# Self-attention: the even steps' probabilities are normalised on ScalarE from step 40 on, and the V fills read the normed input where it lies

## The reference, cut to what matters

```
xn  = rmsnorm(x, gamma1)                              # (8, 256, 128)
q, k, v = xn @ q_w + q_b, xn @ k_w + k_b, xn @ v_w + v_b   # 16 heads of 64
q, k = rope(q), rope(k)
scores = q k^T / 8, causal
attn = softmax(scores)
attn_out = (attn @ v) @ o_w + o_b + xn
an = rmsnorm(attn_out, gamma2)
out = shared_expert(an) + routed_top3_of_31(an) + an + attn_out, then a layernorm
```

## Time and profile before

| | us |
|---|---|
| median of 3 runs | 871.24 (869.53 to 875.28) |
| the profiled execution | 871.48 |
| its span, first to last instruction | 869.7 |
| busy: TensorE, VectorE, ScalarE, POOL | 793.9, 684.6, 574.8, 559.7 |
| self-attention, first to last POOL normalisation | 441.0 to about 735 |
| L989, POOL's normalisation | 64 instructions, 94.2 in total |
| mean granted TensorE clock | 0.985 of full speed |

### The profile page before, as it was taken

How to read it: one execution, slowest core, us unless ns; L and a number is a source line. 1 busy time by engine, 2 the same in 40 slices (tenths; PEclk the granted TensorE clock), 3 DMA queues, 4 the chain that set the end, 5 groups by cost and what they waited for, 6 DMA issues and landing times.

```text
span 869.7 us, 17333 instructions
## 1 busy us (share of the span) xinstructions
PE 793.9 (91%) x5325; PEld 524.2 (60%) x5325; DVE 684.6 (79%) x2434; ACT 574.8 (66%) x1449; POOL 559.7 (64%) x630
## 2 busy tenths in 40 slices
PE   5799999999879999999899999999998888989994
PEld 2344444444456667776556676676666556888763
DVE  3788888889788998889877858868994993565687
ACT  3588778777489999998566646547653566354343
POOL 4888888888662333332476758747796988554562
PEclk9899999999999999999999999999999999999997
DMA  8300000000015111000232212231222236354112
GB/s 242 115 2 1 0 1 0 1 0 1 0 44 152 41 39 46 34 1 2 49 74 71 62 41 68 55 74 39 60 73 69 61 104 186 115 171 144 40 48 58
DMA packets 57850, 51.87 MB, mean 60 GB/s; under 512 B 11586, under 2 KB 43042, under 8 KB 57762
## 3 DMA queue, kind: packets, MB, share of 16 engines
q1 hardware_dynamic: 55394, 46.05, 19.3%
q0 software_dynamic: 2304, 4.72, 1.9%
q10 hardware_dynamic: 64, 0.02, 0.0%
HBM read 21.66 MB, written 12.32 MB: 39 GB/s over the span
## 4 chain that ended last, share of the span: by engine, by line
PE 52%; POOL 19%; DVE 13%; issue 7%; ACT 6%; another core or an unknown queue 1%; ACTq 0%; DVEq 0%; POOLq 0%
PE psum L2092 5%; PE psum L2263 5%; DVE area L1516 4%; PE psum L2125 4%; POOL area L989 4%; PE psum L2109 4%; PE psum L2400 3%; PE psum L2420 3%; PE psum L2460 3%; PE psum L2151 3%; POOL area L898 3%; PE psum L2322 3%; PE psum L2438 3%; POOL slot_in L977 2%; PE psum L1976 2%
## 5 line engine op out<-in xcount | busy, mean ns | idle before, releaser
L989 POOL TENSOR_TENSOR area<-area,rinv 128x512 f32<-128x512 f32 x64 | 94.2, 1473 | 65.2 <-DVE rinv L1837 64.8
L1298 ACT ACTIVATE area<-area,negmax 128x128 f32<-128x128 f32 (+1 forms) x256 | 112.8, 444 | 15.6 <-DVE negmax L1516 15.6
L1145 ACT ACTIVATE area<-area,negmax 128x256 f32<-128x256 f32 x256 | 108.8, 505 | 0.0
L1516 DVE CUSTOM_DVE_ANT_0 area<-psum,area 128x256 f32<-128x256 f32 x256 | 93.2, 420 | 18.3 <-PE psum L2077 17.5
L1505 DVE SCALAR_TENSOR_TENSOR area<-psum,ccol,cs 128x1024 f32<-128x1024 f32 x64 | 81.4, 1272 | 22.8 <-PE psum L2125 22.5
L1516 DVE CUSTOM_DVE_ANT_0 area<-psum,maskc 128x128 f32<-128x128 f32 (+1 forms) x256 | 76.0, 352 | 13.0 <-PE psum L2151 9.5
L2092 PE MATMUL psum<-ident,area 128*128 128x128 f32 x512 | 70.6, 278 | 8.7 <-DVE area L1556 7.3
L2125 PE MATMUL psum<-area,qkw 128*128 128x512 f32 x128 | 71.6, 641 | 6.5 <-DVE area L1505 3.7
L1288 ACT ACTIVATE area<-psum 128x512 f32<-128x512 f32 x32 | 19.1, 598 | 75.7 <-PE psum L2460 67.7
L2092 PEld LDWEIGHTS psum<-ident,area 128*128 128x128 f32 x512 | 56.6, 142 | 18.1 <-issue 11.0
L2438 PEld LDWEIGHTS psum<-ident,area 128*128 128x128 f32 x384 | 44.7, 141 | 36.2 <-issue 25.1
(11 more groups left out here) (315 smaller groups left out, 2091.9 us busy)
## 6 DMA issues: line engine op xcount, KB each, us to landing
area<-area SPq DMA_DIRECT2D x256, 64.0 KB
slot_out<-area SPq DMA_DIRECT2D x17, 256.0 KB
area<-slot_in SPq DMA_DIRECT2D x8, 512.0 KB, 4.1
slot_in<-gate SPq DMA_DIRECT2D x5, 768.0 KB, 4.7
area<-in_L_ffn_re_w SPq DMA_DIRECT2D x14, 256.0 KB
area<-in_mask_BxSxS_ik SPq DMA_DIRECT2D x8, 256.0 KB, 3.8
area<-in_L_attn_W SPq DMA_DIRECT2D x5, 256.0 KB, 6.3
area<-in_x SPq DMA_DIRECT2D x4, 256.0 KB, 3.3
```

Source lines behind the costliest of these rows:

```text
L989: pool.tensor_tensor(p4, p4, rinv[:, u % 4, 0:4].unsqueeze(2).to_broadcast([128, 4, w]), ALU.mult)\
L1145: last = act.activation(P[:, n % 4, r, mm, :], P[:, n % 4, r, mm, :], ACT.Exp, bias=negmax[:, n % 4, r, mm:mm + 1], scale=-1.0)
L1298: last = act.activation(Pc[:, u % 4, r, mm, 0:w], Pc[:, u % 4, r, mm, 0:w], ACT.Exp, bias=negmax[:, u % 4, r, mm:mm + 1], scale=-1.0, accu ...
L1516: return nc.vector.tensor_tensor_reduce(out=dst, in0=scores, in1=mask, scale=scale, scalar=HIGHEST, op0=ALU.add, op1=ALU.min, accum_out=low)
```

## The change

The normalisation of even steps n >= 40 (rounds 8 to 14 of group 2, all even rounds of group 3) moves from POOL to ScalarE: four activations with the inverse row sum as scale, placed behind the copies of step u - 2 and ahead of `keep`. They wait for VectorE's reciprocal and signal a semaphore of their own, `c_pe`, on which TensorE waits in `turn`. The V fill reads `xnT` at the right group; `xcur`, its semaphore and its four copies go. `rp` is given the address that it had.

```
         xnT = shared([128, NG, GT], at=17 * 1024)
         vbb = shared([128, H * HD])
-        xcur = shared([128, GT])
-        rp = shared([128, 2, 4, GT])
+        rp = shared([128, 2, 4, GT], at=20 * 1024 + 512)
...
-        s_xg = sem("self_group_in_place")
+        c_pe = sem("self_even_probs_normalised_by_scalar_engine")
...
+        EVEN_ON_ACT = 5 * SU // 2
...
-                    pool.wait_ge(c_ri, SU * g + u + 1)
-                    p4 = Pc[:, u % 4, :, :, 0:w].rearrange("p r m k -> p (r m) k")
-                    pool.tensor_tensor(p4, p4, rinv[:, u % 4, 0:4].unsqueeze(2).to_broadcast([128, 4, w]), ALU.mult)\
-                        .then_inc(c_pn, 1)
+                    if u % 2 or SU * g + u < EVEN_ON_ACT:
+                        pool.wait_ge(c_ri, SU * g + u + 1)
+                        p4 = Pc[:, u % 4, :, :, 0:w].rearrange("p r m k -> p (r m) k")
+                        pool.tensor_tensor(p4, p4, rinv[:, u % 4, 0:4].unsqueeze(2).to_broadcast([128, 4, w]), ALU.mult)\
+                            .then_inc(c_pn, 1)
...
                             act.activation(PTc[:, v % 2, r, 0:wide], bank[4 + r][:, 0:wide], ACT.Copy).then_inc(c_pt[r], 1)
+                    if u < SU and u % 2 == 0 and SU * g + u >= EVEN_ON_ACT:
+                        act.wait_ge(c_ri, SU * g + u + 1)
+                        for r in range(2):
+                            for mm in range(2):
+                                c = 2 * r + mm
+                                last = act.activation(Pc[:, u % 4, r, mm, 0:128], Pc[:, u % 4, r, mm, 0:128], ACT.Copy,
+                                                      scale=rinv[:, u % 4, c:c + 1])
+                        last.then_inc(c_pe, 1)
                     if u % 2 == 0 and 2 < u < SU:
                         keep(u // 2 - 2)
...
-            def group_in_place(g):
-
-                gg = slice(g, g + 1) if isinstance(g, int) else bass.ds(g, 1)
-                nc.vector.tensor_scalar(xcur[:, :], xnT[:, gg, :].rearrange("p a n -> p (a n)"), 1.0, None, ALU.mult)\
-                    .then_inc(s_xg, 1)
...
-                    if step[2] == 0 and step[1] % HQ == 0:
-                        pe.wait_ge(s_xg, 1 if g is None else g + 2)
+                    gg = 0 if g is None else g if step[1] < HQ else following
...
-                        last = nc.tensor.matmul(dst[:, t2 * 256:(t2 + 1) * 256], xcur[:, k * 128:(k + 1) * 128],
+                        last = nc.tensor.matmul(dst[:, t2 * 256:(t2 + 1) * 256], xnT[:, gg, k * 128:(k + 1) * 128],
...
-                    pe.wait_ge(c_pn, SU * g + u + 1)
+                    n = SU * g + u
+                    if n < EVEN_ON_ACT:
+                        pe.wait_ge(c_pn, n + 1)
+                    elif n % 2:
+                        pe.wait_ge(c_pn, EVEN_ON_ACT + (n - EVEN_ON_ACT + 1) // 2)
+                    else:
+                        pe.wait_ge(c_pe, (n - EVEN_ON_ACT) // 2 + 1)
```

More of the change, by code:

```diff
@@ L1566, in context_step @@
                     dve.wait_ge(s_cw, 16 * CW)
-                    dve.wait_ge(x_read, FILL["rms", 1] + 1)
-                    group_in_place(0)
                 for what, i in head(n):
@@ L1837, in self_attention @@
                         nc.vector.reciprocal(rinv[:, u % 4, 0:4], rsum[:, u % 4, 0:4]).then_inc(c_ri, 1)
-                    if u == SU - 4 and following is not None:
-                        group_in_place(following)
                     steps = spare_steps(u, following, g)
```

## The result

The changed kernel took 887.53 us (median of 4 runs, 880.86 to 888.79) against 871.38 for the kernel before on the same chip (869.53 to 875.28): ratio of the means 1.0164, interval 1.0134 to 1.0194 (every ratio below is one of means). Two later measurements gave 1.0175 (1.0125 to 1.0224) and 1.0177 (1.0140 to 1.0215). It is slower by 16 us where I forecast 7, and above the range's end of 885. The profiled execution took 888.79, its span 887.0, with a mean granted clock of 0.973 (0.985 before).

The account below looks back on a forecast made before the run. From 640 to 660 us it took POOL to bound the kernel, with a new ScalarE loop of 7.6 us per pair of steps replacing it. Stretch terms summed to +6.7 us on 871.48, giving 878 us, range 868 to 885.

Parts of the forecast that it names:

- The loop: Even steps from 40: reciprocal, ScalarE normalisation, keep, odd exponentials, transposed copy, turn, scores, minima, next even reciprocal; 7.6 us per pair.
- the clock: Rival: behind step 56 TensorE stands still and drops to half clock, adding 3 to 4 us, 881 to 883; chance 0.27.
- 40 to 42: Stretch from step 40's reciprocal to step 42's: 10.25 us for the old 8.67, a loss of 1.6 us.
- 48 to 52: Reciprocals of steps 48 to 52: POOL leads and loses one even operation, a gain of 0.85 us against 19.20.
- 56 to 58: Reciprocals of steps 56 to 58: 10.25 us for the old 7.23, a loss of 3.0 us.
- 52 to 56: Reciprocals of steps 52 to 56, with router logits and choosing: 21.0 us for the old 20.76, +0.25.
- 58 to 62: Reciprocals of steps 58 to 62, bound by the loop alone: 16.3 us for the old 12.82, +3.5.
- 46 to 48: Reciprocals of steps 46 to 48, a group's end: TensorE's waits for POOL come back, a gain of 1.3 us.
- 42 to 46: Reciprocals of steps 42 to 46: two loops, 16.4 us for the old 14.66, a loss of 1.7 us.
- Rival A: POOL is the bound and nothing replaces it: seven pairs save 1.06 us each, 7.4 less, 864; chance 0.08.
- B: Rival, about even at 868 to 873: loop nearer 7 us, ScalarE's unexplained 7.95 us wait may vanish; chance 0.17.
- C: Rival: VectorE's scaling and logits shrink by 3 us together beside an idle POOL, giving 875; chance 0.10.

Follow-up runs that it names:

- E8: E2's kernel plus twelve added TensorE transposes between the two halves of each even step's turn from 40 on: ratio 1.0098 to the kernel before.
- E1: Kernel before with only the V fills changed (reading xnT, no copy into xcur), POOL still normalising every step: 863.18 us, ratio 0.9999.
- E11: Changed kernel with only the four even steps 56, 58, 60 and 62 normalised on ScalarE: 871.9 us, ratio 1.0092 to the kernel before.
- E9: Repeat of E2, keep ahead of the normalisation in the changed kernel, in one session with E10: 875.46 us, ratio 1.0130 to the kernel before.
- E10: Repeat of E8, the twelve added transposes per even turn from 40 on, in one session with E9: 872.04 us, ratio 1.0095 to the kernel before.
- E5: The changed kernel measured again, nothing altered: ratio 1.0175 to the kernel before.
- E14: The changed kernel measured once more, nothing altered, in a session with 874.5 us for the kernel before: ratio 1.0177.
- E2: Changed kernel with ScalarE's copy keep moved ahead of the normalisation, nothing else moved: ratio 1.0117 to the kernel before.
- E4: Changed kernel whose ScalarE normalisation uses reciprocals of two steps earlier, so no wait for VectorE (wrong scaling): 857.76 us, ratio 0.9937 to the kernel before.
- E13: Repeat of E3, the late normalisation on ScalarE, with more rounds: ratio 1.0019 to the kernel before.
- E3: Changed kernel with each ScalarE normalisation moved into the next odd round, behind its exponentials and transposed copy: ratio 0.9981 to the kernel before.

## Why the prediction was wrong

**Right.** The loop, and the sign of six of the eight terms that I gave one. N is 1.28 us for the 1.25 that I took the earlier trace rows. E(odd) starts behind N, the even transposes wait for P, POOL's idle time behind R grew. At the full clock the loop has nearly the size worked out: R(42) at 635.10 to R(44) at 643.18 is 8.08 us, where 7.6 + 0.6 = 8.2 was forecast, though R(44) to R(46) is 9.02. (Of its parts, 4 x 0.497 is 1.99 and not 1.97, which changes nothing.) E8, with TensorE at the full clock from 680 us on and `keep` out of the loop, took 9.88 us from R(56) to R(58) and 15.19 from R(58) to R(62); the forecast less 0.5 for each `keep` is 9.75 and 15.3. E1 bears out the zero for the V fills, E11 that the stretch behind step 56 needs no history.

**The step that failed: the clock, which I let fall only behind step 56, and there as a rival with a chance of 0.27.** The forecast's terms are sized at 2.4 GHz. Timeline of TensorE in the changed kernel, behind R(40), at the change of groups and behind R(58):

```profile
626.83 1.70 PE L2124 MATMUL psum<-area,qkw 128*128 128x512 f32 x2
628.33 1.06 PE L2442 MATMUL psum<-ident,area 128*128 128x128 f32 x4
...
672.27 6.76 PE L2320 MATMUL psum<-ow,area 128*128 128x128 f32 x32 [3.10 <-ACT area L1289]
...
733.80 0.69 PE L2442 MATMUL psum<-ident,area 128*128 128x128 f32 x2 [1.37 <-ACT area L1317]
734.42 2.08 PE L2149 MATMUL psum<-area 64*128 64x256 f32 x8
736.43 2.07 PE L2130 MATMUL psum<-vw,area 128*128 128x256 f32 x4
```

and before, at that change of groups:

```profile
667.25 3.81 PE L2322 MATMUL psum<-ow,area 128*128 128x128 f32 x32 [2.30 <-ACT area L1288]
```

Term by term:
- 40 to 42, 1.5 us too small: projection 1.70 for 1.13, turn 1.06 for 0.60, scores 1.79 for 1.13, together +1.7.
- 48 to 52, 2.8 too small: the output projection took 6.76 for 3.81, +2.95, and R(48) to R(49) grew from 3.29 to 6.25.
- 56 to 58, 2.1 too small: from R(56) to the first minimum 7.54 us (724.51) where 6.2 was forecast, the scores alone +0.95; from there to R(58) 4.83 for 4.03, since the slot bases wait for TensorE's matmuls behind values of 1.97 us (1.09 at the full clock).
- 52 to 56 and 58 to 62, 1.15 and 1.0 too small: both hold a stretch at half clock (702 to 705, 733 to 740); that is all that puts them down to the clock.

These add up to 8.5 of the 10.6 us by which the sum fell short. That the clock costs time and isn't only a companion is shown by E9 and E10, for 3.4 us net in a kernel that stands still less. The changed kernel's own runs fit: of the eight runs of E5 and E14, the four with clocks of 0.964 to 0.967 took 890.5 to 893.1, the other four with 0.969 to 0.975 took 885.4 to 890.8. The share of 8.5 in the changed kernel itself is read from rows, not from an experiment, and two parts of it overlap with other causes: the projection of 40 to 42 stands behind the values, on the second arm, and the 2.95 us at the change of groups follow the pause that is not shown to be the change's.

**What I left out: the second arm.** I wrote that the copy out of PSUM stands behind N, priced its 0.5 us, and didn't ask who waits for it. TensorE's values of the even steps do, with everything that is queued behind them. E2 and E9 put it at about 4 us, by a ratio across sessions; in their traces, with the full clock, R(40) to R(42) took 9.97 and 9.98 us for 11.74 in the changed kernel. It can't be added to the clock's 8.5: its pauses are what the falls of the clock follow in two of five stretches. Arm and clock together can be measured within one session: E8, without the arm and nearly without the falls, took 882.7 us, the changed kernel (E5) 890.6, 7.9 more, although E8 has the twelve times twelve transposes on top.

**46 to 48, 1.4 too small.** I let waits for POOL come back, 1.3 us. R(46) to R(47) grew by that much (4.33 to 5.62) instead, and R(47) to R(48) fell by 1.2. I read that as relief which came one step later, behind a loop that was still closed; no run tests it. The 0.7 by which 42 to 46 fell short, at the full clock, stays open too.

**Rival A** (all relief, 864) did not come true in the changed kernel, but E4 shows a gain once the wait is off: 5 us, not 7, and a part of it may be the clock's. The Trainium skill's rule that I set beside the sum (ScalarE: Activation LUTs, Rules for kernel authors: multiplies belong to VectorE) fits the sign of the result but not its cause: in E4 the same multiplies on ScalarE cost nothing. **B** lived on the 7.95 us wait of ScalarE going away; it is still there, 8.75 us:

```profile
671.53 0.60 ACT L1289 ACTIVATE area<-psum 128x512 f32<-128x512 f32 x1 [8.75 <-remote]
```

**C**, relief on VectorE, was right in substance, and too small to turn the result. VectorE's scaling and the logits' last operation, in the changed kernel:

```profile
691.33 2.97 DVE L1664 TENSOR_SCALAR rT<-xT,rms 128x128 f32<-128x128 f32 x1
...
703.69 0.29 DVE L1742 TENSOR_TENSOR area<-area 128x124 f32<-128x124 f32 x1
```

They took 4.00 and 3.56 before. R(51) to R(52) fell from 9.15 to 8.11; E4 has 8.10 there and E1, with POOL's full load, 9.11. The page of the Trainium skill that I named with C (GPSIMD Engine Reference) fits the direction: fewer POOL operations, shorter VectorE operations beside them. Whether these VectorE operations are of the kind that it names, no run here shows.

## What to carry to other kernels

Before an operation that waits is put on a queue, list every instruction behind it and every engine that waits for each; here one of three was missed, and it was worth as much as half of the forecast. If the wait closes a loop, work that is free elsewhere on that engine counts in full: ask for a place where the operand has been there for a while. And where a forecast has TensorE stand still some microseconds per round at an uneven pace, size its terms at both levels of the clock, in the first such round as much as in the last.

## What the runs showed that I had not expected

- Adding work made a kernel faster: 144 transposes more, 0.4% less time (E9, E10).
- Wait and work are not additive: -0.6% and +0.5% apart, +1.7% together.
- The kernel before took 863.1 and 863.6 us in two sessions, 871.4, 871.7 and 874.5 in three others. In the slower ones ScalarE has a pause of 7.8 to 9.6 us at the change of groups with the releaser "remote" (kernel before and changed, E5 to E8, E13, E14), and a second of 2.3 to 4.9 us between 855 and 876; in all eight runs of the faster sessions neither is there. What it waits for the profile does not name, and no run here tells.
- The clock falls without the change too: the kernel before has 0.62 from 732 to 736 us, E1 about half from 704 to 712, and E3 and E4 have no such stretch between 664 and 748 us.
